# Cross attention of layer 3 with 8-wide values per head, sums from a block of ones, and the division on the 128-wide result

## What is computed

```python
qh = (q @ w_q + b_q).reshape(b, -1, h, dk).transpose(0, 2, 1, 3)   # h = 16, dk = 8
kh = (k @ w_k + b_k)...; vh = (v @ w_v + b_v)...                   # k, v: the context
qh = _rope(qh); kh = _rope(kh)
scores = jnp.einsum('bhqd,bhkd->bhqk', qh, kh) / math.sqrt(dk)
scores = jnp.where(mask, scores, jnp.finfo(scores.dtype).min)
attn = jax.nn.softmax(scores, axis=-1)
out = jnp.einsum('bhqk,bkhd->bqhd', attn, vh)
return out.reshape(b, -1, h * dk) @ w_o + b_o
...
x = x + jnp.tanh(g_xattn[3]) * _L3_xattn_ref(_layernorm(x), ctx, ctx, mask, ...)
x = x + jnp.tanh(g_ffn[3]) * _L3_ffn_ref(_layernorm(x), ...)
```

## Time and profile before

| what | value |
|---|---|
| time, median of 3 runs | 1049.45 us (1048.04 to 1050.45) |
| span of the profiled execution | 1057.6 us, 19542 instructions |
| PE busy | 919.4 us, 87% |
| DVE busy | 785.7 us, 74% |
| ACT busy | 557.7 us, 53% |
| POOL busy | 490.0 us, 46% |
| first score of layer 3's loop | 927.71 us from the span's start |
| last update of the loop begins | 1019.67 us |

### The profile page before, as it was taken

How to read it: one execution, slowest core, us unless ns; L and a number is a source line. 1 busy time by engine, 2 the same in 40 slices (tenths; PEclk the granted TensorE clock), 3 DMA queues, 4 the chain that set the end, 5 groups by cost and what they waited for, 6 DMA issues and landing times.

```text
span 1057.6 us, 19542 instructions
## 1 busy us (share of the span) xinstructions
PE 919.4 (87%) x6337; PEld 655.6 (62%) x6337; DVE 785.7 (74%) x2080; ACT 557.7 (53%) x1494; POOL 490.0 (46%) x451
## 2 busy tenths in 40 slices
PE   6898985888778999869997598988989999989987
PEld 4787533767578989727775243434437677768774
DVE  6889999999756777769998376777734744589982
ACT  4675456886444445724443156766764233445533
POOL 5444553555066564635556777574530600024430
PEclk9999896999879999969999659989999999999998
DMA  9300000000111111410000322222102000000001
GB/s 324 149 1 1 2 6 1 1 1 1 41 39 39 41 40 33 109 66 1 0 1 0 107 67 62 82 76 62 31 1 101 1 1 1 1 2 2 1 1 40
DMA packets 29828, 40.55 MB, mean 38 GB/s; under 512 B 11468, under 2 KB 25036, under 8 KB 29228
## 3 DMA queue, kind: packets, MB, share of 16 engines
q1 hardware_dynamic: 27244, 34.28, 10.3%
q0 software_dynamic: 2496, 5.16, 1.9%
HBM read 31.44 MB, written 7.82 MB: 37 GB/s over the span
## 4 chain that ended last, share of the span: by engine, by line
PE 27%; issue 14%; POOL 7%; DVE 5%; ACT 3%; SPq 1%; DMA 0%; DVEq 0%; POOLq 0%; ACTq 0%
POOL att L1787 6%; PE ps L1163 4%; PE ps L829 4%; PE ps L1135 4%; PE ps L819 4%; PE ps L1147 3%; PE ps L793 1%; PE ps L1249 1%; PE ps L1257 1%; DVE rs L2124 1%; PE ps L1101 1%; DVE stats L2001 0%; SPq L570 0%; PE ps L1106 0%; DVE U L2029 0%
## 5 line engine op out<-in xcount | busy, mean ns | idle before, releaser
L1787 POOL TENSOR_TENSOR att<-att,ri 128x1232 f32<-128x1232 f32 x64 | 169.3, 2645 | 190.5 <-DVE ri L2130 190.5
L793 PE MATMUL ps<-VW,PT 128*128 128x128 f32 (+3 forms) x1280 | 157.6, 278 | 17.5 <-DVE x L2145 16.0
L793 PEld LDWEIGHTS ps<-VW,PT 128*128 128x128 f32 (+1 forms) x1280 | 148.4, 192 | 35.2 <-DVE x L2145 28.3
L1369 ACT ACTIVATE PT<-ps 128x512 f32<-128x512 f32 x128 | 70.6, 594 | 89.5 <-PE ps L766 88.7
L766 PE MATMUL ps<-W,att 128*128 128x128 f32 (+1 forms) x640 | 86.9, 282 | 16.2 <-POOL att L1787 14.7
L1761 POOL TENSOR_TENSOR rstd<-ve,minus_half 128x4 f32<-128x4 f32 x38 | 38.8, 1039 | 114.2 <-DVE ve L2016 97.7
L900 PE MATMUL ps<-PT,att 128*128 128x128 f32 x624 | 80.8, 285 | 8.5 <-issue 8.4
L829 PEld LDWEIGHTS ps<-U,att 128*128 128x128 f32 x512 | 66.3, 191 | 33.1 <-issue 29.1
L766 PEld LDWEIGHTS ps<-W,att 128*128 128x128 f32 (+1 forms) x640 | 72.7, 143 | 22.3 <-POOL att L1787 15.5
L2581 DVE CUSTOM_DVE_ANT_0 C<-ps,cmaskb 128x512 bf16<-128x512 f32 (+1 forms) x128 | 71.1, 555 | 20.7 <-PE ps L1135 18.0
L2581 DVE CUSTOM_DVE_ANT_0 U<-ps,cmaskb 128x384 bf16<-128x384 f32 (+1 forms) x128 | 53.9, 421 | 41.8 <-PE ps L1135 41.5
(11 more groups left out here) (432 smaller groups left out, 2105.6 us busy)
## 6 DMA issues: line engine op xcount, KB each, us to landing
U<-in_ffn SPq DMA_DIRECT2D x1, 6176.0 KB, 23.2
U<-split SPq DMA_DIRECT2D x144, 32.0 KB
W<-split SPq DMA_DIRECT2D x144, 32.0 KB
W<-in_packed SPq DMA_DIRECT2D x1, 2162.5 KB, 23.5
U<-in_ffn SPq DMA_DIRECT2D x1, 2060.0 KB, 9.7
U<-in_moe SPq DMA_DIRECT2D x1, 2048.0 KB, 7.3
split<-VBD SPq DMA_DIRECT2D x4, 384.0 KB, 2.9
split<-W SPq DMA_DIRECT2D x4, 384.0 KB, 2.7
```

The costliest lines, as they stand in the source:

```text
L793: q = mm(attended(s, t), PT[0:m, t.slot(2), c, :], batch(VW, t.group)[0:m, c * D:(c + 1) * D], start=(c == 0), stop=(c == NC - 1))
L1369: go(PT[:, t.slot(2), 4 * k:4 * k + 4, :].rearrange("p c n -> p (c n)"), ps[:, k0 + k, :], ACT.Copy).then_inc(probsT, 1)
L1787: tt(p, p, over_keys(ri[:, t.slot(2), :]), ALU.mult).then_inc(probs, 1)
```

## The change

The values are no longer multiplied with the output projection beforehand. They are spread over only 308 columns per batch (`VBG`), turned into `VN` (`value_blocks`), and the loop, now `narrow`, computes unnormalised outputs: per tile 12 products that each write 32 partitions of PSUM (four heads x 8 columns; four column groups side by side) and 12 more of the same kind with a block of ones in place of the values, which give each head's sum of exponentials. The scores read the queries from `FT` directly, and the mask is added by products of 32 rows. Per pair of tiles, ACT copies outputs and sums, PE turns the sums, DVE inverts them, POOL spreads the inverse over the 8 columns of a head, PE turns that back, DVE multiplies (128 x 256), PE projects, DVE adds to x (128 x 256). The output bias, times the gate, is added to x by POOL after each batch is normalised. The block of ones (96 columns) joins the first group of constants. The exponentials are turned in 12 blocks (8 of 128 columns, 4 of 52, `REST`), copied in three ACT instructions. The diff, cut to its core:

```diff
+    "a": [("ident", P), ("hm", H), ("hg", H // RG), ("ones", 3 * 32), ("desc", E), ("gates", 8), ("ctxT", CK),
...
+        VBG = VBD[:, :].rearrange("p (b n) -> p b n", b=B)
+        VN = VW_flat[:, 0:B * 3 * P].rearrange("p (b c n) -> p b c n", b=B, c=3)
+        share = cmaskb[:, 0:P]
...
-                        rotate(B - 1)
-                        pe.wait_ge(roped, B - 1)
-                        pe.wait_ge(q_sb, 2 * B)
-                    if s == X3 and t.n + 2 < B:
-                        fold_values(s, w(f"{LAYER[s]}wo"), t.n + 2)
...
+            def value_blocks(s, b):
+                pe.wait_ge(vbd, BLOCKS0[s] + B)
+                if b == 3:
+                    pe.wait_ge(vw_sb, BLOCKS0[s] + 2)
+                bank = b % 3
+                for c in range(2):
+                    pe.transpose(ps[:, bank, c * P:(c + 1) * P], VBG[:, b, c * P:(c + 1) * P], ident)
+                pe.transpose(ps[0:REST, bank, 2 * P:3 * P], VBG[:, b, 2 * P:GK], ident).then_inc(vw_ps, 1)
+            def narrow(s):
+                def score(t):
+                    b = t // TB
+                    if t % TB == 0:
+                        pe.wait_ge(roped, b + 1)
+                    wait(pe, shifted, n0 + t + 1)
+                    for g in range(RG):
+                        rows = rows_of_group(g)
+                        mm(ps[:, g, 0:GK], FT[rows, t * P:(t + 1) * P], KBG[rows, b, :], start=True, stop=False)
+                    for g in range(RG):
+                        rows = rows_of_group(g)
+                        m = mm(ps[:, g, 0:GK], share[rows, :], nb3[rows, b, g * GK:(g + 1) * GK], start=False, stop=True)
+                    m.then_inc(scores, 1)
+                def turn_piece(t, k):
+                    p = 3 * (n0 + t) + k
+                    if k == 0:
+                        pe.wait_ge(expd, n0 + t + 3)
+                    wait(pe, probsT, p + 2)
+                    e = att[:, t % SLOTS_OF_SCORES, :]
+                    if k < 2:
+                        for i in range(4):
+                            at = (2 * k + i // 2) * GK + i % 2 * P
+                            q = pe.transpose(ps[:, 4 + p % 2, i * P:(i + 1) * P], e[:, at:at + P], ident)
+                    else:
+                        for g in range(RG):
+                            q = pe.transpose(ps[0:REST, 4 + p % 2, g * P:(g + 1) * P], e[:, g * GK + 2 * P:(g + 1) * GK], ident)
+                    q.then_inc(probsT_ps, 1)
+                def weigh(t):
+                    q, i = divmod(t, 2)
+                    if i == 0 and q >= 2:
+                        pe.wait_ge(x_new, XNEW0[s] + 2 * (q - 1))
+                    if t == 0:
+                        pe.wait_ge(vw_sb, BLOCKS0[s] + B + 1)
+                    for a in range(2):
+                        for c in range(3):
+                            pe.wait_ge(probsT, 3 * (n0 + t) + (5 if c < 2 else 6))
+                            for g in range(RG):
+                                m = P if c < 2 else REST
+                                lhs = VN[0:m, t // TB, c, rows_of_group(g)] if a == 0 else w("ones")[0:m, 32 * c:32 * c + 32]
+                                z = mm(ps[rows_of_group(g), tail_bank(q), (2 * a + i) * P:(2 * a + i + 1) * P], lhs,
+                                       PT[:, t % 2, 2 * g + c, :] if c < 2 else PTR[0:REST, t % 2, g * P:(g + 1) * P],
+                                       start=c == 0, stop=c == 2)
+                    z.then_inc(n_weighed, 1)
+                def turn_sums(q):
+                    pe.wait_ge(rowsum, n0 + 2 * q + 2)
+                    for i in range(2):
+                        z = mm(sums_by_query(q)[:, i * H:(i + 1) * H], ORS[:, q % 2, (2 + i) * P:(3 + i) * P],
+                               ident.rearrange("p (h d) -> p h d", d=HD)[:, :, 0], start=True, stop=True)
+                    z.then_inc(n_sumsT, 1)
+                def turn_inverse(q):
+                    pe.wait_ge(staged, n0 + 2 * q + 2)
+                    for i in range(2):
+                        z = pe.transpose(right(q)[:, i * P:(i + 1) * P], inverse[:, q % 2, i * P:(i + 1) * P], ident)
+                    z.then_inc(n_spread, 1)
+                def project(q):
+                    pe.wait_ge(probs, n0 + 2 * q + 4)
+                    for i in range(2):
+                        z = mm(left(q)[:, i * P:(i + 1) * P], onT[:, q % 2, i * P:(i + 1) * P], w(f"{LAYER[s]}wo"), start=True, stop=True)
+                    z.then_inc(attn_out, 2)
+                pe.wait_ge(kbd, KEYED[s] + 1)
+                pe.wait_ge(tables_set, 5)
+                for k in range(NT + 4):
+                    if k < NT:
+                        score(k)
+                    if k == 0:
+                        rotate(B - 1)
+                    if 0 <= k - 2 < NT:
+                        weigh(k - 2)
+                    if 0 <= k - 1 < NT:
+                        turn_piece(k - 1, 0)
+                        turn_piece(k - 1, 1)
+                    if k >= 5 and k % 2 == 1:
+                        project((k - 5) // 2)
+                    if k >= 4 and k % 2 == 0:
+                        turn_inverse((k - 4) // 2)
+                    if k >= 3 and k % 2 == 1 and (k - 3) // 2 < NT // 2:
+                        turn_sums((k - 3) // 2)
+                    if 0 <= k - 1 < NT:
+                        turn_piece(k - 1, 2)
...
-            pe.wait_ge(kv_chain, 5)
-            fold_values(X3, w("3wo"), 0)
+            for b in range(3):
+                value_blocks(X3, b)
             starts(pe, X3)
             rotate(0)
             q3(1)
             turn_x3(2)
             rotate(1)
-            fold_values(X3, w("3wo"), 1)
+            value_blocks(X3, 3)
             q3(2)
             turn_x3(3)
             rotate(2)
             q3(3)
             pe.wait_ge(turned_sb, TURN0[X3] + B + 1)
-            cross(X3)
+            narrow(X3)
...
+            def narrow(s, scale):
+                def exponent(t):
+                    act.wait_ge(shifted, n0 + t + 2)
+                    e = att[:, t % SLOTS_OF_SCORES, :]
+                    go(e, e, ACT.Exp, scale=scale).then_inc(expd, 1)
+                def take_sums(q):
+                    act.wait_ge(n_weighed, m0 + 2 * q + 2)
+                    if q >= 2:
+                        act.wait_ge(probs, n0 + 2 * q)
+                    go(ORS[:, q % 2, :], ps[:, tail_bank(q), :], ACT.Copy).then_inc(rowsum, 2)
+                def evacuate(t, k):
+                    p = 3 * (n0 + t) + k
+                    if t >= 2:
+                        act.wait_ge(n_weighed, m0 + t - 1)
+                    act.wait_ge(probsT_ps, p + 7)
+                    if k < 2:
+                        go(PT[:, t % 2, 4 * k:4 * k + 4, :].rearrange("p c n -> p (c n)"), ps[:, 4 + p % 2, :], ACT.Copy)\
+                            .then_inc(probsT, 1)
+                    else:
+                        go(PTR[0:REST, t % 2, :], ps[0:REST, 4 + p % 2, :], ACT.Copy).then_inc(probsT, 1)
+                for k in range(1, NT + 3):
+                    if k - 1 < NT:
+                        exponent(k - 1)
+                    if k >= 3 and k % 2 == 1:
+                        take_sums((k - 3) // 2)
+                    if k - 1 < NT:
+                        for piece in range(3):
+                            evacuate(k - 1, piece)
...
-                tt(heads(VBD3_at[b]), v3_s[:, b * KEYS:(b + 1) * KEYS].unsqueeze(1).to_broadcast([P, H, KEYS]),
-                   over_keys(w("hm")), ALU.mult).then_inc(vbd, 1)
+                tt(VBG[:, b, :].rearrange("p (h k) -> p h k", k=KEYS),
+                   v3_s[:, b * KEYS:(b + 1) * KEYS].unsqueeze(1).to_broadcast([P, H // RG, KEYS]),
+                   w("hg").unsqueeze(2).to_broadcast([P, H // RG, KEYS]), ALU.mult).then_inc(vbd, 1)
+            pool.memset(share, 1.0 / 32).then_inc(tables_set, 1)
             pool.wait_ge(ld["e"], 32)
+            pool.tensor_scalar(w("3bo"), w("3bo"), tg[:, 3:4], None, ALU.mult).then_inc(x_biased, 1)
...
-            roots(X3)
-            cross(X3)
+            def spread_inverse(s):
+                for q in range(NT // 2):
+                    pool.wait_ge(recip, tiles_before(s) + 2 * q + 2)
+                    pool.tensor_copy(inverse[:, q % 2, :].rearrange("p (i h d) -> p i h d", i=2, d=HD),
+                                     ri2[:, q % 2, :, :].unsqueeze(3).to_broadcast([P, 2, H, HD])).then_inc(staged, 2)
+            def add_bias(s, b):
+                pool.wait_ge(s_xn, TB * (ROUND0[s] + b + 1))
+                pool.wait_ge(x_biased, 1)
+                xb = x[:, b * TB:(b + 1) * TB, :]
+                tt(xb, xb, w(f"{LAYER[s]}bo").unsqueeze(1).to_broadcast([P, TB, D]), ALU.add).then_inc(x_biased, 1)
+            for b in range(B):
+                root(ROUND0[X3] + b, b)
+                if b >= 1:
+                    add_bias(X3, b - 1)
+            add_bias(X3, B - 1)
+            spread_inverse(X3)
...
+            def narrow(s):
```

(38 more changed lines are left out.)

99 lines of the change are left out of this document (50 added, 49 removed).

## The result

| what | before | changed |
|---|---|---|
| median of the runs on one chip | 1050.47 us (6 runs, 1048.04 to 1051.12) | 1043.28 us (6 runs, 1035.99 to 1046.18) |
| ratio, 95% interval | | 0.992 (0.9892 to 0.9949) |
| span of the profiled execution | 1057.6 us | 1042.8 us (its own time 1044.64) |

The change makes the kernel faster by 0.8% (0.5 to 1.1%); the medians lie 7.2 us apart where 12.4 were forecast. The time is inside the forecast range.

The account below looks back on a forecast made before the run. DVE set the loop's turn, PE 0.3 us behind; afterwards PE binds. Head -4.3, loop -7.2, end -1.1, constants +0.2 sum to -12.4 us: 1049.45 - 12.4 = 1037.0 us, range 1029 to 1046 (own 1032 to 1042).

Parts of the forecast that it names:

- Head: Before the loop: shorter folds on PE let DVE's rotations start earlier, first largest at 924.95 instead of 929.24, 4.3 us gained.
- PE's turn: In the loop: PE's new list takes 4.71 us in odd turns, 4.26 in even, mean 4.49, PE-bound.
- rival 1: In `weigh`: the column groups' weight loads follow each other and show, 0.227 us per group instead of 0.111; 1058 us, 10%.
- Rival 2: In `weigh`: part of the weight loads shows, 0.14 us per group, 0.35 per tile; 1041 to 1043 us, 12%.
- rival 6: In `weigh`: matmul issue binds at about 62 ns each, 1.65 us more per tile; 1063 us, 2%.
- rival 5: In the loop: the turn stays at DVE's or PE's 4.9 us, head and end even out; 1049 us, 4%.
- Fall of the clock in the loop's head: Early in the loop: PE's gaps bring one stretch at 1.2 GHz, charged 1.7 us; bounds none or two falls.
- Tail: From the last largest to the last update: 13.8 us instead of 15.03, 1.1 gained after a 0.1 longer last update.
- POOL's tables: In the experts' stage: tables for the values shrink where POOL isn't waited for, so nothing gained.
- rival 4: In the loop: hand-overs bind, each turn losing 0.5 us where a wait meets a busy ACT; 1044.5 us, 6%.
- Rival 3: In the loop: PE turns out shorter and the score banks' floor binds, 4.1 us per turn; 1031.5 us, 12%.
- First constants: At the kernel's start: 96 more columns, 48 KB, land 0.2 us later (0 to 0.35), uncovered.

Follow-up runs that it names:

- the shortened folds alone: Kernel before, with layer 3 multiplying only two of its ten blocks of values with the output projection per batch; ratio 0.9975.
- 128 rows everywhere: Changed kernel, with the third block of `weigh` using 128 rows instead of 52, spare value rows zeroed; ratio 0.9838, again 0.9829 (1035.46 us).
- the fillers: Unread bf16 products in PE's gaps, added to the changed kernel with 128 rows in every `weigh` product; ratio 0.9842, again 0.9794 (1031.55 us).
- four long tables: Changed kernel plus four extra POOL multiplications of 128x1232 ahead of its small value tables; ratio 0.9928.
- three long tables: Changed kernel plus three extra POOL multiplications of 128x1232 ahead of its small value tables; ratio 0.9923.

## Why the prediction was near, and where it failed

- **Head: right.** 3.9 us gained for 4.3 forecast (11.16 us against 10.8), and the shortened folds alone bring 3.1 of it.
- **PE's turn: one term wrong.** In the odd turn the scores take 0.86 us (0.89 forecast), and transposes, the pair's work and the last change of shape 2.27 (1.31 + 0.88 + 0.10 = 2.29). `weigh` with the way out of its shape took 1.85 and not 1.33 + 0.20 = 1.53. The 1.33 was right (1.45 with 128 rows everywhere, so the way out costs 0.12), the weights stay hidden, and rivals 1, 2 and 6 fall. Missing were three changes of the row count, 0.39 together. Rival 2 named nearly that sum (0.35 per tile, 1041 to 1043 us) for another reason: its number is near by luck. In the even turn the third piece starts 3.72 us after the score with 128 rows everywhere (951.82 - 948.10), to the hundredth as forecast, but partly by luck: the transposes start at 2.31 instead of 2.42, and ACT's copy brings PE on 1.41 later instead of 1.30 (the terms written down give 1.24; 0.06 is not accounted for). It is 4.11 in the changed kernel (948.46 - 944.35), again 0.39 more. So turns are 4.99 and 4.67 instead of 4.71 and 4.26, 4.81 on average, not far from rival 5's 4.9, but because PE's new list is long and not because the old one stays. Eleven full turns cost 52.9 us instead of 49.1, the three before them 0.8 more.
- **Fall of the clock in the loop's head: the charge was a guess of the right kind.** 1.7 us were charged. In the profiled execution the fall (3.4 us from 920.5 on) lies under DVE's fourth rotation and the start of the second turn and costs nothing: these turns take 5.00 and 3.95, as they do at full clock with the fillers. In the one with four long tables it lasts 6.8 us and lies on the third turn, 7.27 us instead of 4.61. The loop gained 4.2 us of 7.2: 3.8 and 0.8 lost by the turns, 1.7 not spent.
- **Tail: forecast -1.1, measured +0.1.** Two prices were wrong: the row changes in the last two `weigh`s (14.30 us without them), and a clock at 1.2 GHz from 1002.4 us on, where PE has waited for POOL and DVE. The clock's part is 0.5 us: with three long tables it fell only at the very end of the tail, which took 14.62. With both away it takes 13.78, near the forecast's 13.8.
- **Behind the stage: missed, 1.1 us.** I took the feed-forward's start as unchanged. The clock falls behind PE's gaps in the tail: the 48 small matmuls take 5.17 us at a granted clock of 0.50, against 2.84 at full clock. With fillers in those gaps they take 2.84 again. Part of the 2.3 us comes back, since in the kernel before the clock falls later (granted 0.61 over 1029 to 1033) and slows the work there.
- **POOL's tables: "nothing" was wrong, by 2.7 us in favour.** I asked only who waits for POOL, and not whom POOL holds up.
- **DVE, ACT, POOL: right in size.** `scale` 0.42 (0.43 forecast), the spread 0.40 (0.47 to twice that), the largest and shift unchanged. The bias additions take 1.09 to 1.47 us, not 0.94, and nothing waits for them. No engine but PE sets a full turn, and rival 4 falls, though its 1044.5 us is near the measured time. Rival 3's floor exists at 3.95 but PE doesn't reach it.
- **First constants: +0.2 not seen.** PE starts at 6.0 us in both.
- **"8.15 us below the span": wrong.** An execution's time lies 1.8 us above its span for the changed kernel (1042.8 and 1044.64) and 2.2 above it for the kernel before (1062.4 and 1064.64). So the profiled execution before, with a span of 1057.6, took near 1060 us, longer than the timed ones. The forecast, 1049.45 - 12.4, doesn't hang on it.

Sum by the profiles: head -3.9, loop -4.2, tail +0.1, behind +1.1, experts' end -2.7, together -9.6 us, against -12.4 forecast and -7.2 between the medians (the ratio's interval is -5.3 to -11.3). So the sign and over half of the size were right; the largest miss is the 3 us of the loop, made up, by luck, by a gain of 2.7 us that I had put at nothing.

## What to carry to other kernels

Pad a ragged last block of a matmul with zeros up to the row count of its neighbours: on PE 128 rows cost as much as 52 here (0.34 and 0.35 us), while each change of the row count costs 0.13 us, which adds up to 4 us of the stage between the profiles and to 6 at the same clock. Before a step is costed at nothing because nobody waits for its engine, look at what DVE does with two SBUF inputs at that moment: a long POOL instruction holds it up. Compare stretches between fixed points of the program, not spans: the same kernel's spans differ by up to 14 us for reasons outside the change.
